# A two-stage decoder kernel: weights, first normalisation and first queries of the cross stage moved into the end of the self stage

## The reference

```python
x = x + _L0_attn_ref(_layernorm(x, axis=-1), L0_attn_qkv_w, L0_attn_qkv_b, L0_attn_out_w, L0_attn_out_b)
x = x + _L0_xattn_ref(_layernorm(x, axis=-1), ctx_1024, ctx_1024, mask_BxS2_bf1, L0_xattn_Wq, L0_xattn_bq, L0_xattn_Wk, L0_xattn_bk, L0_xattn_Wv, L0_xattn_bv, L0_xattn_Wo, L0_xattn_bo)
x = x + _L0_ffn_ref(_layernorm(x, axis=-1), L0_ffn_Win, L0_ffn_bin_, L0_ffn_W1, L0_ffn_b1, L0_ffn_W2, L0_ffn_b2, L0_ffn_Wout, L0_ffn_bout)
```

## Time and profile before

| what | value |
|---|---|
| median of 3 runs | 1825.08 us (1824.74 to 1825.36) |
| the profiled execution | 1824.81 us |
| its span in the trace | 1823.0 us |
| PE busy | 1686.1 us (92%) |
| DVE busy | 1523.1 us (84%) |
| ACT busy | 1083.7 us (59%) |
| POOL busy | 1018.6 us (56%) |
| mean granted clock of TensorE | 0.972 |

### The profile page before, as it was taken

The page is one execution under the profiler, slowest core; times in us unless marked ns, Lnnn a source line. Parts: engine busy times, 40 slices in busy tenths (PEclk is TensorE's granted clock), DMA queues, the critical chain, the costliest instruction groups (busy, mean ns, idle before and its releaser), DMA issues.

```text
span 1823.0 us, 37774 instructions
## 1 busy us (share of the span) xinstructions
PE 1686.1 (92%) x13848; PEld 1392.5 (76%) x13848; DVE 1523.1 (84%) x2097; ACT 1083.7 (59%) x3456; POOL 1018.6 (56%) x721
## 2 busy tenths in 40 slices
PE   6899999999999999963799999999999999999996
PEld 5778888888888888842577777778777787777874
DVE  6798888888888888773478998889988899888887
ACT  4434444444444444322567887778877788777884
POOL 3167777766666777673344645546455464544521
PEclk9999999999999999986799999999999999999997
DMA  5401111111111111042011110111101112011101
GB/s 212 136 24 47 41 34 43 46 46 46 46 46 46 46 46 47 24 81 77 24 44 50 61 60 26 60 61 61 64 23 61 61 61 64 21 61 61 38 25 47
DMA packets 72794, 98.76 MB, mean 54 GB/s; under 512 B 22208, under 2 KB 30528, under 8 KB 72640
## 3 DMA queue, kind: packets, MB, share of 16 engines
q1 hardware_dynamic: 71056, 96.09, 16.2%
q10 hardware_dynamic: 1584, 0.61, 0.2%
HBM read 59.66 MB, written 37.03 MB: 53 GB/s over the span
## 4 chain that ended last, share of the span: by engine, by line
PE 27%; ACT 12%; DVE 9%; issue 5%; ACTq 0%; DVEq 0%
PE ring L1269 12%; ACT prob_c L1493 10%; DVE g_sb L1617 5%; PE sc L1297 5%; PE ring L1274 3%; PE ring L1309 3%; PE ring L1356 2%; PE sc L1289 2%; PE sc L1269 1%; DVE q L1804 1%; ACT relu L1473 1%; DVE g_sb L1614 1%; DVE gT L1627 1%; ACT gT L1483 1%; ACT pT L1461 1%
## 5 line engine op out<-in xcount | busy, mean ns | idle before, releaser
L412 PE MATMUL qb<-wqkv,xT 128*128 128x512 f32 x2304 | 551.3, 393 | 6.1 <-DVE wqkv L869 6.1
L412 PEld LDWEIGHTS qb<-wqkv,xT 128*128 128x128 f32 x2304 | 429.5, 189 | 93.5 <-DVE wqkv L869 6.3
L1493 ACT ACTIVATE prob_c<-sc,ntop 128x128 f32<-128x128 f32 x1024 | 363.4, 391 | 8.2 <-DVE ntop L1645 6.5
L1221 POOL TENSOR_TENSOR rstd<-vare,half_c 128x1 f32<-128x1 f32 x64 | 35.1, 549 | 456.6 <-DVE vare L1699 456.6
L1493 ACT ACTIVATION_READ_ACCUMULATOR prob_c<-sc,ntop 128x1 f32 x1024 | 235.7, 230 | 0.0
L330 POOL TENSOR_TENSOR prod_pool<-v,prob 128x1024 f32<-128x1024 f32 x64 | 180.6, 2822 | 74.7 <-DVE prob L795 69.5
L1269 PE MATMUL ring<-wqkv,aT_c 128*128 128x512 f32 x768 | 193.5, 401 | 10.5 <-DVE aT_c L1600 9.6
L501 PE MATMUL ob<-wout,aT 128*128 128x512 f32 x768 | 192.0, 399 | 11.2 <-DVE aT L825 11.2
L581 ACT ACTIVATE v<-qb 128x512 f32<-128x512 f32 x64 | 38.4, 599 | 260.3 <-PE qb L412 251.8
L1269 PE MATMUL ring<-xT_c,wqkv 128*128 128x512 f32 x768 | 185.4, 401 | 1.5 <-DVE xT_c L1600 1.5
L581 ACT ACTIVATE qk<-qb 128x512 f32<-128x512 f32 x128 | 76.1, 596 | 177.1 <-PE qb L412 177.1
(11 more groups left out here) (137 smaller groups left out, 3349.8 us busy)
## 6 DMA issues: line engine op xcount, KB each, us to landing
x_tile<-in_x SPq DMA_DIRECT2D x16, 1024.0 KB, 5.3
x_scratch<-xres SPq DMA_DIRECT2D x16, 1024.0 KB, 4.5
x_tile<-x_scratch SPq DMA_DIRECT2D x16, 1024.0 KB, 5.2
out<-x SPq DMA_DIRECT2D x64, 256.0 KB, 2.0
kt<-k_scratch SPq DMA_DIRECT2D x16, 512.0 KB, 3.2
v_c<-v_scratch SPq DMA_DIRECT2D x16, 256.0 KB, 3.6
raw<-in_wqkv SPq DMA_DIRECT2D x3, 1024.0 KB, 8.8
ctx<-in_ctx SPq DMA_DIRECT2D x1, 1024.0 KB, 8.4
```

The lines of the kernel that those rows point to most:

```text
L412: last = nc.tensor.matmul(qb[g % 4][:, :], xT[p][a][:, k, t * P:(t + 1) * P], wqkv[b][:, k, c * D:(c + 1) * D], start=(n == 0), stop=(n == ...
L1493: last = nc.scalar.activation(prob[:, h, :], sc[g][:, (h % 4) * C:(h % 4 + 1) * C], ACT.Exp, bias=ntop[:, h:h + 1], accum_out=total[:, t % ...
```

## The change

- The weights `wq` and `wo` are loaded in step 15 instead of 16, into a staging place of their own (`stage_w`, over `xT` of even blocks, which block 14 was the last to use). They are split in step 15: `wq` by ACT behind the take of group 6 and by DVE behind `score_sum(1)`, `wo` in four pieces behind the takes of groups 8 to 11 and, on DVE, between `take_x1(2)` and `take_x1(3)`. `win` and `wf` are loaded in step 15 too and split in step 16.
- The first block of x1 and its statistics are loaded in step 15, behind `wq` and `wo` on SP's queue and ahead of `win` and `wf`. Step 15's stores stand behind all these loads.
- Step 16 has an order of its own on PE, ACT and DVE. It holds the first cross block's normalisation (POOL `first_norm`, ahead of its `weigh`), its transposes, its four queries and their splits. The output projections of block 15 are no longer interleaved with the transposes of later tiles.
- Block 15's statistics are taken by DVE (`bn_stats`) right behind each `take_x1`, instead of by ACT in step 17.
- SP does not wait for the last stores at the end of the self stage. It waits for them in the cross stage, behind the loads of keys, mask and values and ahead of 12 small DMAs, which move there from ACT's queue. The 13th, `bq`, is issued at the program's start.
- The cross stage begins with step 0. The residual sums of its first block stand at the head of POOL's step 0, ahead of the second block's normalisation, and wait for the small DMAs.

```diff
-    for j in range(-1, last + 1):
+    for j in range(last + 1):
...
-                if is_step(j, TILES):
-
-                    sp.wait_ge(qk_sum, R * TILES)
+                if is_step(j, TILES - 1):
+
+                    sp.wait_ge(qkv_psum, N_QKV * (TILES - 1))
                     sp.wait_ge(xt_psum, R * TILES)
-                    for n, (loads, _, _) in enumerate(pieces):
-                        for dst, part in loads:
-                            sp.dma_start(dst, part).then_inc(in_w[n], 16)
+                    for n in (0, 1):
+                        sp.dma_start(*pieces[n][0][0]).then_inc(in_w[n], 16)
...
             run_self_steps(sp, step)
-            for p in range(2):
-                sp.wait_ge(x1_out[p], 16 * (TILES // 2))
-                sp.wait_ge(st_out[p], 16 * (TILES // 2))
...
+            def first_norm():
+                pool.wait_ge(keep["x1_in"], 32)
+                pool.wait_ge(res_done, TILES)
+                pool.wait_ge(xn_done, R * TILES)
+                for i in range(R):
+                    nc.gpsimd.tensor_tensor(x[1][:, i, :], x[0][:, i, :], keep["st"][:, i, 0:1].to_broadcast([P, D]),
+                                            ALU.add).then_inc(x0m_done, 1)
+                    pool.wait_ge(x0m_done, i + 1)
+                    nc.gpsimd.tensor_tensor(x[1][:, i, :], x[1][:, i, :], keep["st"][:, i, 1:2].to_broadcast([P, D]),
+                                            ALU.mult).then_inc(x0n_done, 1)
...
+                if is_step(j, TILES):
+                    for i in range(R):
+                        first_norm_T(i)
+                    first_queries(0)
+                    first_queries(1)
+                    first_queries(2)
+                    attn_T(0)
+                    first_queries(3)
+                    output_projection(j, 0)
+                    for t in range(1, R):
+                        attn_T(t)
+                        output_projection(j, t)
+                    return
...
+                if is_step(j, TILES):
+                    x1_sum(0)
+                    x1_sum(1)
+                    x1_sum(2)
+                    for i in range(R):
+                        first_norm_hi(i)
+                    x1_sum(3)
+                    x1_mean()
+                    x1_square(0)
+                    x1_square(1)
+                    first_queries_hi(0)
...
+            load_ctx(0, 0)
+            for p in range(2):
+                sp.wait_ge(keep["x1_out"][p], 16 * (TILES // 2))
+                sp.wait_ge(keep["st_out"][p], 16 * (TILES // 2))
+            for dst, part in small:
+                sp.dma_start(dst, part).then_inc(in_small, 16)
...
+                if is_step(j, 0):
+                    pool.wait_ge(in_small, 16 * len(small))
+                    for i in range(R):
+                        residual(i, -1)
```

More of the change, by code:

```diff
@@ L110, in sem @@
             return stack.enter_context(nc.semaphore(name))
-        ident, wqkv, bout = keep["ident"], keep["wqkv"], keep["bout"]
+        ident, wqkv = keep["ident"], keep["wqkv"]
+        with ExitStack() as early:
+            stage_w = [early.enter_context(nc.sbuf_tensor(f"stage_w{h}", [P, DK, D], F32)) for h in range(2)]
+        with ExitStack() as early:
+            q_first = [early.enter_context(nc.sbuf_tensor(f"q_first{h}", [P, DK, R * P], F32R)) for h in range(2)]
+        keep["q"] = q_first
+        xT = [[sb(f"xT0_{h}", [P, DK, R * P], F32R) for h in range(2)]]
+        bout = sb("bout", [P, D])
         with ExitStack() as early:
@@ L302, in step @@
                                  st_dram[0, 0:R * P, :].rearrange("(t p) c -> p t c", p=P)).then_inc(keep["x1_in"], 16)
+                    for n in (2, 3):
+                        for dst, part in pieces[n][0]:
+                            sp.dma_start(dst, part).then_inc(in_w[n], 16)
                 if has(j, -1):
@@ L883, in step @@
                     dve.wait_ge(k_out, 16 * 2 * R)
+                if is_step(j, TILES):
+                    softmax_norm()
+                    for i in range(R):
+                        first_norm_lo(i)
+                    weigh_mul(0)
+                    weigh_sum(0)
+                    first_queries_lo(0)
+                    weigh_mul(1)
+                    a_lo(0)
+                    weigh_sum(1)
+                    first_queries_lo(1)
+                    first_queries_lo(2)
+                    take_x1(0)
+                    last_stats_of(0)
+                    a_lo(1)
+                    first_queries_lo(3)
+                    split_lo(2)
+                    split_lo(3)
+                    take_x1(1)
+                    a_lo(2)
+                    last_stats_of(1)
+                    take_x1(2)
+                    a_lo(3)
+                    last_stats_of(2)
+                    take_x1(3)
+                    last_stats_of(3)
+                    last_variance()
+                    return
+                if is_step(j, TILES + 1):
+                    return
                 softmax_norm()
@@ L935, in step @@
                     variance_of(j + 2)
+                if is_step(j, TILES - 1):
+                    for k in range(DK):
+                        split_lo(1, k)
                 take_x1(3)
@@ L1172, in step @@
             def step(j, p):
-                if has(j, 1) and not is_step(j, -1):
+                if has(j, 1):
                     at = tokens((j + 1) * (R * P), R * P)
-                    wait_each(sp, (xn_done, R * (j + 1)), (res_done, R * (j + 1)))
+                    wait(sp, xn_done, R * j)
+                    wait(sp, res_done, R * (j + 1))
                     sp.dma_start(x1[:, :, :], x1_flat[at, :].rearrange("(t p) d -> p t d", p=P)).then_inc(x1_in, 16)
@@ L1588, in step @@
                         take_hi(j, "q", m, q[0][:, m, :], ACT.Identity, bias=bq[:, m:m + 1])
-            for dst, src in small:
-                act.dma_start(dst, src).then_inc(in_small, 16)
             run_steps(act, step)
```

191 lines of the change are left out of this document (127 added, 64 removed).

## The result

The changed kernel takes 1798.88 us (median of 4 runs, 1798.29 to 1803.03), against 1825.22 us of the kernel before (4 runs): a ratio of 0.9856, 95% interval 0.9844 to 0.9868, 26.3 us less. The forecast was 1796.2 in a range of 1788 to 1804: the time lies in the range, 2.7 us above the forecast. The profiled execution took 1798.63 us, its span 1796.8.

A forecast was written before the change was run, and what follows sets the result against it. DVE and POOL were taken to bound the self stage's tail, waits the hand-over, a four-engine chain step -1. First scores 30.35 us earlier, less 1.5, turned 1824.81 into 1795.96; the median's 0.27 gave 1796.2, range 1788 to 1804.

The forecast's parts named there:

- The sum: Whole kernel: first scores 30.35 us earlier, less 1.5 for the low clock, 28.85 in all; profiled execution 1795.96.
- the keys: Cross stage's start: keys and mask land 9.7 us after 844.6, scores at 854.5, with 849.5 and 859.3 as ends.
- the time behind the first scores: Step 0 and later: tile 0's scores at the low clock give 1.5 us back; nothing counted after that.
- Step 15: Early loads and splits: step 16's softmax starts at 803.3 instead of 801.25, 2.0 us later, 8.2 at the upper end.
- The 8 us of room: Step 15: wq, issued at about 752.5, lands at 767, 8 us ahead of ACT's take of group 6 at 774.25.
- Step 16: Last self-stage tiles, with first norm and queries brought in: take_x1(3) ends at 840.9 instead of 844.4, 3.5 us earlier.
- The rule of the Trainium skill: Keys count as landed only after the statistics: scores at 851.7 to 856.5, time 1793.4 to 1798.2; excludes rival 1.
- Rival 1: Cross stage's start: keys are not held up and land after 4.5 to 5 us; 1791 us; chance 0.15.
- Rival 2: Step 16: PE becomes the bound at a low clock, queries 16.2 us instead of 10.9; 1801.5, up to 1807; chance 0.15.
- Rival 3: Hand-over: the branch out of the stage is still held until the stores have landed; 1798 to 1804 us; chance 0.07.
- Rival 4: Step 0: second block's norm comes 15 to 25 us later, losing 10 to 20; slower only beyond 916; chance 0.02.
- the signs of being wrong: Profile after: ACT waiting for in_wq in step 15, PE for POOL in step 0, or scores before 850 or after 860.

The follow-up runs named there:

- e4: Kernel before with only the early loads of the weights and first x1 block, and the splits of wq and wo, in step 15; 1815.12 us.
- e3: Changed kernel with the transposes of tiles 2 and 3 set ahead of the projections of tiles 1 and 2 in step 16; 1797.06 us.
- e1: Changed kernel with the last two stores of the statistics issued behind the loads of keys, mask and values; 1792.31 us.
- e7: Changed kernel with each block's statistics stored as 128 pieces of 32 bytes instead of 512 of 8; 1791.96 us.
- e11: Changed kernel with statistics in 32-byte pieces, transposes set ahead, and 20 added matmuls between the last projection and the first scores; 1789.97 us.
- e8: Changed kernel with the last statistics' stores behind the keys and step 16's transposes set ahead of the projections; 1790.54 us.
- e2: Changed kernel with SP's wait for the stores put back at the end of the self stage; 1804.50 us.
- e5: Changed kernel with 38 matmuls added on PE between the last projection and the first scores; 1797.88 us.
- e6: Changed kernel with block 15's statistics taken by ACT behind all four take_x1, as before the change, instead of by DVE; 1801.73 us.
- e10: Changed kernel with both statistics in 32-byte pieces and step 16's transposes set ahead of the projections; 1788.65 us.

## Why the prediction was right, and where it was off

**The sum.** The forecast for the profiled execution was 1795.96, and it took 1798.63: 2.67 us more. In the terms of the prediction: 1.16 is there before step 15, 0.63 of it with the execution and 0.53 with the program, which the sum has no term for; the self stage ended at 844.5 as forecast (844.6), so relative to that offset it came 1.2 better; the keys cost 1.3 more; the time behind the first scores grew by 2.9 where 1.5 were counted, 1.4 more. 1.16 - 1.2 + 1.3 + 1.4 is 2.7.

**Step 15** was forecast to cost 2.0 us and cost 2.5: `take_x1(3)` ends at 804.91, less the offset 803.75, against 801.25. In e4, which has the same loads and splits, step 15 cost 1.1 (801.91 for the row at 800.64, less 0.19 of offset). What e4 lacks there is POOL's first norm, which runs from 794.03 to 803.8 beside DVE's split of `wo`. DVE's rows of the changed kernel, and then of e4, whose POOL is idle:

```profile
797.29 1.30 DVE L871 TENSOR_TENSOR prob<-logit,top 128x256 f32<-128x256 f32 x1
...
799.12 5.27 DVE L945 SCALAR_TENSOR_TENSOR wqkv<-stage_w,vscale,wqkv 128x512 fp32r<-128x512 f32 x4
```

```profile
797.27 2.07 DVE L861 SCALAR_TENSOR_TENSOR wqkv<-stage_w,vscale,wqkv 128x512 fp32r<-128x512 f32 x3
800.43 0.75 DVE L861 SCALAR_TENSOR_TENSOR wqkv<-stage_w,vscale,wqkv 128x512 fp32r<-128x512 f32 x1 [1.10 <-ACT wqkv L604]
```

The four pieces take 5.27 us beside the norm and 2.82 without it. The prediction's 5.93 for them came from a row beside a busy POOL, so its 2.0 came near; but the norm, which it calls hidden, accounts by these rows for the difference between 1.1 and 2.5. No run takes the norm away by itself.

The loads went wrong in a way that did not matter. They were to be issued at about 752.5, when block 14's products end. SP reached them only at 758.12: ahead of them on its queue stands the store of block 13's x1, which waits for DVE until 757.09, and a store of statistics. `wq` then took 15.2 us behind that store. I had read the loads' own condition and not what stands ahead of them. It landed at 773.3, 6 us later than I had worked out, and ACT began its split at 775.90, as it came to it, with no wait. The 8 us of room had shrunk to 2.6:

```profile
775.90 1.91 ACT L657 ACTIVATE wqkv<-stage_w 128x2048 fp32r<-128x2048 f32 x1
```

The same queue also held SP for 12.84 us on the issue of `win` (two DMAs; `wf` took 2.65 more), which nobody was waiting for:

```profile
758.12 1.06 SPq L303 DMA_DIRECT2D stage_w<-in_wq  x1
...
762.39 12.84 SPq L315 DMA_DIRECT2D xn<-in_win  x2
```

**Step 16** went nearly as laid out, and its parts can be read beside the forecast (in brackets), without taking off the 1.16: softmax ready 806.5 (804.9), queries from 808.97 (807.4), `attn_T(0)` 819.40 (818.3), `a_lo(1)` done 827.9 (827.9), last `take_x1` done 841.4 (840.9). POOL's norm ended at 803.8 (799 to 805), ahead of the softmax; POOL's weighing ended at 828.9 (830), covered by 6.8 us. DVE's rows:

```profile
804.31 0.68 DVE L937 TENSOR_TENSOR xres<-ob,xres 128x512 f32<-128x512 f32 x1
...
806.44 2.48 DVE L956 TENSOR_TENSOR xT<-qb,xT 128x512 fp32r<-128x512 f32 x4
808.83 3.18 DVE L895 TENSOR_TENSOR prod<-v,prob 128x2048 f32<-128x2048 f32 x1
...
820.86 0.69 DVE L915 TENSOR_TENSOR aT<-tb,aT 128x512 fp32r<-128x512 f32 x1 [0.98 <-ACT aT L612]
...
840.72 0.69 DVE L937 TENSOR_TENSOR xres<-ob,xres 128x512 f32<-128x512 f32 x1 [2.29 <-PE ob L558]
```

DVE waits 2.29 us for PE at the last sum, so the new order on PE, and no longer DVE, sets the last tiles; e3 showed the price, 2.7 us at the stage's end, or 2.2 without that run's earlier start.

**The keys** were the widest bound of the sum, 4.9 to 14.5 us, and the middle, 9.7, was taken. They took 10.5 (and the mask 10.5 from an issue 0.5 later). The mechanism is shown by e1 and e7: with the small pieces behind the keys, or joined, it is 3.8. What is not shown is whether the queue matters: no run stores the statistics from another engine's queue. This step is right in kind and 1.3 short in size. The rule of the Trainium skill (DMA: Bandwidth & Descriptors, Queues, rings and completion order), that the completion count is written only after the same DMA engine's earlier writes, is in agreement with these landings: the statistics landed at 854.6, the keys at 855.0, and the time of 1798.88 is 0.7 above the upper end that was worked out from it. It is not proved by them, since the windows also show the bytes themselves moving at 35 to 86 GB/s, and no run here separates a late count from late data. The first scores themselves, at 855.72, lie inside the 851.7 to 856.5 that were worked out with it; the 0.7 comes from the other terms.

**The time behind the first scores** is the step that failed in its reasoning. I priced tile 0's scores (1.5, measured 0.80 + 2.69 for 0.51 + 1.46, which is right) and counted nothing after. But the clock also rises later: in the third scores it is still low for a while (2.05 against 1.61 us in the kernel before), and the first transpose of block 1 stands 33.73 us behind the first scores instead of 31.83. That is 1.9 of the 2.9 us, 0.4 more than was priced, and it is the clock's work: in e11, in which PE comes warm to the scores, the transpose stands 31.25 us behind them. The other 1.0 us gathers behind that transpose, and warmth at the first scores doesn't take all of it away. The ten kernels that have the whole change take 906.75 to 907.35 us from there to the end (changed kernel 907.35, e11 906.84), the three that don't 906.30 to 906.42 (before 906.32). So 0.3 us at the least comes with the program, up to 1.0 in the changed kernel, and what does it was not tested. That e11's whole time behind the scores (938.09) equals the kernel before's (938.15) is a coincidence: it is 0.6 us quicker up to the transpose and 0.5 slower behind it.

**The rivals.** Rival 1, keys not held up, is refuted by 10.5 us; the 1791 that it gave is close to what e1 and e7 got by making it true (1792.31 and 1791.96). Rival 2, the low clock in step 16, did not happen in the profiled execution (0.92), but it did to a smaller size in e1, e3 and e8, each time in the projection of tile 1 (5.49, 4.46 and 4.36 us for 3.02), so the mechanism is there, in one product and not in all. The three queries ahead of it, 36 matmuls, took 9.90 to 11.23 us in the ten executions (10.59 here); in the three that took over 11 (e1, e2, e7) x1 was stored 1.6 us later or more. Rival 3, a branch held by the stores, is refuted: the keys were issued at 844.53, 10 us before the statistics had landed. Rival 4, the second block's chain, did not bite:

```profile
862.70 4.95 POOL L1363 TENSOR_TENSOR xr<-x_tile,bo 128x512 f32<-128x512 f32 x4 [17.92 <-DMA hinge<-in_w]
873.50 1.04 POOL L1354 TENSOR_TENSOR xn_c<-x_tile,st_c 128x512 f32<-128x512 f32 x1 [5.86 <-DMA st_c<-st_scratch]
```

The first tile is normalised at 875.7 (forecast 882), and its transpose is at 889.45: 13.8 us of room where 4 to 8 were forecast, since each link was priced at its upper end: the four sums took 4.95 us and not 7.1, and the small DMAs began at 854.63 and not at 856.3. In e8, where the scores come 9 us earlier, 5.2 us are left, and in e1 2.8. Of the signs of being wrong that the prediction names, none showed in the changed kernel.

**What stays open.** Why the clock falls in tile 1's projection in some executions and not in others; why, without added matmuls, the first transpose of block 1 stands anywhere from 33.05 to 34.98 us behind the first scores; what in the program costs 0.53 us from block 0 to block 13 and 0.3 to 1.0 us behind the first transpose of block 1; and why executions differ by up to 0.8 us at block 0's store.

## What to carry to other kernels

A wait that is removed at a stage's end pays in full only if what is queued behind it is not held by the same transfer. Before taking a wait away, read how long the transfer takes that it waits for, and put what the next stage needs first ahead of it, or make that transfer quick. Here 6.6 to 6.9 of the 11 us that the wait's removal had freed were got only by that. Many pieces of a few bytes were dear for what stood behind them on the queue, however few the bytes: their layout in a scratch that only this kernel reads is free to choose. And before an offset between two traces is put down to the run, look whether every kernel with the edit has it.

## What the runs showed of the hardware

- A store of 4 KB in 512 pieces of 8 bytes landed after 7.8 to 12.6 us (before) and 10.8 to 13.8 (changed kernel); the same 4 KB in 128 pieces of 32 bytes after 2.3 to 5.4 (e7). A store of 1 MB on the same queue took 4.4 us (e1).
- Behind two of the first, a load of 512 KB landed after 10.5 to 12.3 us (changed kernel, e3, e5, e6), behind two of the second after 3.8 (e7); a load of 1 MB right behind one such store after 15.2 and 8.1.
- SP was held for 12.84 us on the issue of two DMAs of 128 KB behind such a store, three loads of 1 MB and a load of 4 KB in 8-byte pieces. In e10, with the larger pieces, the same two issues took 5.98 us.
- Four splits of 128x512 on DVE took 5.27 us beside POOL's norm (changed kernel) and 2.82 with POOL idle (e4).
- After 15 us without matmuls the granted clock was at its lower level, 0.50 or 1.2 GHz, and stayed there for the first two tiles' scores; it rose in the third's. After 8.7 and 8.8 us without them (e7, e10) it was the same. With matmuls up to the first scores (e11) it was at 1.00 for these and fell again behind them (0.50 at the second tile's), as in the kernel before.
